# Attention: how the 32 couples of maxima of the next head are placed in the 16 groups of a head

## The reference, cut to what matters

```python
q = _split_heads(x @ Wq + bq, h)          # 16 heads of 64
k = _split_heads(x @ Wk + bk, h)
v = _split_heads(x @ Wv + bv, h)
pattern = jnp.einsum('bhid,bhjd->bhij', k, q) * scale
prob = jax.nn.softmax(pattern, axis=-2)
out = jnp.einsum('bhis,bhid->bhsd', prob, v)
...
return concat @ Wo + bo
```

## Time and profile before

| | us |
|---|---|
| median of 3 runs | 4512.2 |
| lowest and highest | 4512.07, 4518.56 |
| the profiled execution | 4520.46 |
| its span, first to last instruction | 4518.6 |
| start of the exponentials of head 0 and end of the last of head 31 | 108.4, 2910.8 |
| busy PE, DVE, ACT, POOL over the span | 4197.6, 3211.1, 3013.1, 2739.8 |

### The profile page before, as it was taken

One profiled execution on the slowest core, in us unless ns is written; L12 is line 12 of the kernel. 1 busy time (PEld: TensorE's weight loads), 2 busy tenths in 40 slices (PEclk: granted clock), 3 DMA queues, 4 the chain that ended last, 5 costly groups with the idle time before them and its releaser, 6 DMA issues.

```text
span 4518.6 us, 66192 instructions
## 1 busy us (share of the span) xinstructions
PE 4197.6 (93%) x23992; PEld 2418.2 (54%) x23992; DVE 3211.1 (71%) x4408; ACT 3013.1 (67%) x4371; POOL 2739.8 (61%) x1215
## 2 busy tenths in 40 slices
PE   7999999999999999999999999779998897999898
PEld 5444444444444444444444444357776675777675
DVE  5877878778778787787887788446664545666455
ACT  5877777778777787787786777646665444666442
POOL 2867778678766786786777777734553333454332
PEclk7999999999999999999999999979999998999999
DMA  2000000100010000001000100010000000000001
GB/s 82 23 21 29 21 21 15 35 21 15 21 33 16 21 24 25 21 15 35 20 16 21 34 16 16 10 61 1 1 1 21 18 1 19 1 1 1 1 1 38
DMA packets 100859, 89.47 MB, mean 20 GB/s; under 512 B 51092, under 2 KB 74088, under 8 KB 100584
## 3 DMA queue, kind: packets, MB, share of 16 engines
q1 hardware_dynamic: 100584, 85.75, 6.5%
HBM read 64.21 MB, written 4.46 MB: 15 GB/s over the span
## 4 chain that ended last, share of the span: by engine, by line
PE 42%; POOL 26%; DVE 12%; issue 11%; ACT 7%; POOLq 1%; DMA 1%; ACTq 0%; SPq 0%; DVEq 0%
POOL accp L780 23%; PE psum L1620 8%; PE psum L1790 6%; PE psum L1608 5%; PE psum L1572 5%; DVE mx L1216 4%; PE psum L1836 2%; PE psum L1920 2%; ACT lp L1029 2%; PE psum L1850 2%; POOL accp L776 2%; PE psum L1933 2%; PE psum L1827 2%; PE psum L1549 2%; PE psum L1557 1%
## 5 line engine op out<-in xcount | busy, mean ns | idle before, releaser
L780 POOL TENSOR_TENSOR accp<-accp,prob 128x1024 f32<-128x1024 f32 x704 | 1783.3, 2533 | 352.9 <-ACT prob L951 270.2
L1216 DVE TENSOR_REDUCE mx<-psum 128x1 f32<-128x512 f32 x1984 | 1276.9, 685 | 341.0 <-PE psum L1572 295.0
L951 ACT ACTIVATE prob<-psum 128x1024 f32<-128x1024 f32 x1024 | 1031.2, 1016 | 539.5 <-PE psum L1608 535.5
L1620 PE MATMUL psum<-prob,vv 128*64 128x512 f32 x4096 | 993.3, 606 | 0.0
L939 ACT ACTIVATE psum<-nm_all 128x1024 f32<-128x1024 f32 x832 | 855.8, 1029 | 26.3
L1572 PE MATMUL psum<-kh,qh 64*128 64x512 f32 x2048 | 494.6, 473 | 119.3 <-DVE mx L1216 113.4
L1572 PEld LDWEIGHTS psum<-kh,qh 64*128 64x128 f32 x2048 | 206.4, 185 | 607.0 <-DVE mx L1216 523.8
L811 POOL TENSOR_TENSOR lp<-lp,lrcp 128x1024 f32<-128x1024 f32 x128 | 242.6, 1895 | 448.6 <-DVE lrcp L1377 448.6
L1620 PEld LDWEIGHTS psum<-prob,vv 128*64 128x64 f32 x4096 | 248.7, 136 | 486.1 <-issue 391.1
L1608 PE MATMUL psum<-qh,kh 64*128 64x512 f32 x2048 | 419.8, 399 | 5.4 <-ACT psum L939 5.0
L1608 PE MATMUL psum<-ql,kh 64*128 64x512 f32 x2048 | 412.3, 391 | 0.0
(11 more groups left out here) (218 smaller groups left out, 6835.7 us busy)
## 6 DMA issues: line engine op xcount, KB each, us to landing
nm_all<-nm_rows SPq DMA_DIRECT2D x128, 256.0 KB, 3.7
kl<-kl SPq DMA_DIRECT2D x64, 256.0 KB, 3.8
wqk<-L_attn_Wq SPq DMA_DIRECT2D x64, 64.0 KB, 2.0
rot_l<-const_rot SPq DMA_DIRECT2D x2, 2048.0 KB, 8.6
out<-lpT SPq DMA_DIRECT2D x32, 128.0 KB, 1.7
wqkv_l<-L_ffn_wqkv SPq DMA_DIRECT2D x4, 768.0 KB, 9.7
w_l<-L_ffn_w SPq DMA_DIRECT2D x4, 618.0 KB
wqk<-L_attn_Wk SPq DMA_DIRECT2D x32, 64.0 KB, 2.1
```

The costliest lines, as they stand in the source:

```text
L780: pool.tensor_tensor(acc_p[cp][:], first[:], prob[kt % PRING][:], ALU.add).then_inc(pool_sum, 1)
L951: act.activation(prob[t % PRING][:], psum[:, S_BANK + 2 * (t % 2):S_BANK + 2 * (t % 2) + 2, :].rearrange("p a b -> p (a b)"), ACT.Exp, sca ...
L1216: dve.tensor_reduce(mx4[:, e, qt, c:c + 1], ps, AX_X, ALU.max).then_inc(ring_free, 1)
L1620: mm = pe.matmul(psum[j * DH:(j + 1) * DH, O_BANK, :], vv[:, kt, s * DH:(s + 1) * DH], prob[t % PRING][:, j * T:(j + 1) * T], start=(kt == ...
```

## The change

The weights go, and the places no longer depend on what else the head has to do. The counts are written out: two couples in most groups, one in group 0 and in group 11 (the first behind the middle sum), three in groups 6, 8, 13 and 14, none in group 15. All heads with maxima get

- 1 2 2 2 2 2 3 2 3 2 2 1 2 3 3 0

```diff
-        def max_places(outs):
-            weight = [4] * (GROUPS - 1) + [0]
-            weight[0] = 1
-            weight[SUM0_GROUP + 1:SUM0_GROUP + 3] = [0, 2]
-            for g in outs:
-                weight[g] = 3
-            return [-(-COUPLES * sum(weight[:g + 1]) // sum(weight)) for g in range(GROUPS)]
+        def max_places():
+            counts = [2] * (GROUPS - 1) + [0]
+            counts[0] = counts[SUM0_GROUP + 1] = 1
+            for g in (6, 8, GROUPS - 3, GROUPS - 2):
+                counts[g] = 3
+            assert sum(counts) == COUPLES
+            return [sum(counts[:g + 1]) for g in range(GROUPS)]
...
-            placed = max_places([*outs, *turns])
+            placed = max_places()
```

## The result

| | before | after |
|---|---|---|
| median, us | 4515.4 (4 runs) | 4629.1 (4 runs, 4623.2 to 4632.2) |
| span of the profiled execution | 4518.6 | 4627.9 |
| start of the exponentials of head 0, end of the last of head 31 | 108.4, 2910.8 | 108.8, 3020.4 |
| from one head to the next, even heads (median) | 88.2 | 91.7 |
| odd heads | 88.3 | 92.5 |

The changed kernel takes 1.025 times the time of the kernel before, interval 1.0237 to 1.0262. A fourth execution of the kernel before has moved its median from 4512.2 to 4515.4 us. All of the difference lies in the attention: between the two profiled executions it is 109.3 us from mark to mark of the third line, and 109.3 in the span.

The account below looks back on a forecast made before the run. PE bounds attention, and DVE's reductions where couples crowd. From 4512.2 us, +67 for the moved couples (+68, head 14 about -1) and +45 for the clock gave 4624 us (+2.5%), range 4545 to 4675.

Parts of the forecast that it names:

- Ahead of the middle sum: Attention up to group 10: three couples fewer bring its values earlier, -2.4 us in even heads, -1.0 in odd.
- The price of two twos in a row: Attention: two successive groups of two couples cannot keep 3.92 us each but take 4.16, 0.24 more.
- Behind the middle sum: Groups 11 and 12, all 30 heads: idle PE gap of 2.6 to 2.8 us, values of group 12 +3.2 us.
- Ahead of the turn: Group 14 gets a third couple, its tail waits for one more reduction: +1.2 us even heads, +0.3 odd.
- Sum without the clock: Attention: +2.0 us in each of 14 even heads and +2.5 in each of 16 odd ones, +68 us.
- The lower bound of the parts: Lowest total of the per-head terms in attention: 30 x 0, within bounds of 0 to 120 us.
- Head 14: This head already has a gap of 5.54 us and gets a shorter one: about -1 us.
- The clock: Behind the new gap PE's clock falls in half of 30 heads, 3 us each: +45 us, bounds 0 and 90.
- Rival C: Attention: all heads lose the clock behind the new gap, +90 us, 4669 us; chance 0.13.
- B: Attention: no head loses the clock behind the new gap, 4579 us; chance 0.24.
- E: Attention: POOL becomes the bound, adding at most 1 us a half, 4654 us or so; chance 0.08.
- D: Attention: spread pays in full, -3.6 us per head ahead of the sum, stall under 3.0; 4507 us; chance 0.13.

Follow-up runs that it names:

- e2: The changed kernel with the third couple of group 6 placed in group 5 instead; 4581.7 us, 1.0152 times the kernel before.
- e5: The kernel before with the third couples of groups 7 and 9 moved to groups 11 and 12, head 14 unchanged; 4577.3 us, 1.0139 times the kernel before.
- e4: The changed kernel with POOL's additions cut to the first 512 of 1024 columns; 4546.9 us, 1.0071 times the kernel before.
- e3: As e2, plus ten matmuls that nobody reads in group 12 ahead of its first couple; 4560.9 us, 1.0101 times the kernel before.

## Why the prediction was right, point by point

The point was 4624 us and the median is 4629. The mechanism is as forecast but for the clock, whose share came out near the forecast by luck. The parts, against the changed kernel with its idle stretches filled, where the clock takes nothing:

| per head, us | predicted | even | predicted | odd |
|---|---|---|---|---|
| values of group 10 | -2.4 | -2.46 | -1.0 | -0.77 |
| groups 11 and 12 | +3.2 | +3.01 | +3.2 | +3.01 |
| group 14 | +1.2 | +1.30 | +0.3 | +0.33 |
| whole head | +2.0 | +1.86 | +2.5 | +2.60 |

- *Ahead of the middle sum.* Right in both kinds of head, and for the reasons given. The gain of group 5 in even heads (3.91 instead of 5.05) is gone in group 6 (6.3 instead of 5.16), DVE's addition ending 1.1 us behind POOL's in both kernels. In odd heads the addition of tile 11 waits longer and group 6 takes 6.3. The price of two twos in a row was set at 4.16 a group; groups 2 to 5 of the odd heads took 3.91 to 4.84, 4.3 on average, and where two follow each other without a DVE addition in between, the second takes about 4.47 and the next 4.0. The mean was nearly right, the pattern was not seen. Group 10 shows it in both kinds of head (4.45).
- *Behind the middle sum.* The mechanism is as forecast, row by row. The gap is 2.50 us, not 2.6 to 2.8; the reciprocal starts at +3.2 (799.03 - 795.82), not +3.4.
- *Ahead of the turn.* Right in size and place: 5.21 in both kinds of head.
- *Sum without the clock.* +68 was predicted; 69 were measured with the fillers. The lower bound of the parts is not 0 as stated: -3.4 + 2.5 + 0.3 in odd heads gives -0.6 each, about -8 us in all. Nothing hung on it.
- *Head 14.* It gained 3.5 us, where -1 was predicted. What was left out is that the clock no longer falls there, which the prediction itself had priced at 3 us. With the fillers head 14 takes 98.8 us: the ten matmuls cost 2.9 us there, and they are in the 69.
- *The end of head 30.* The kernel before had a second long fall there, which the prediction did not see and which is gone in the changed kernel:

```profile
2842.15:2848.95 6.80, 4.87 (x18) 2.69 (x20) 2.85 (x1) 0.84 (x1) 1.79 (x1) 0.50 0.44 148
```

Head 30 took 87.9 us before and takes 88.1 now, while the other even heads got 3.5 longer.
- *The clock.* +45 was predicted for the 30 heads and 48 measured, but that agreement is owed to two errors that cancel. The step that failed is "I let it fall in half of the 30 heads: 15 x 3". There were 30 falls, in all heads with the new order but two (heads 0 and 14; head 29 had two). And each cost 1.6 us, not 3: the clock stayed low for 3.4 us here, where it had for 6.8 behind the gap in head 14 from which the price was taken. Also the place was wrong: 22 of the 30 came behind the wait of 1.43 us in group 6, a place for which the sum had priced the wait and not the clock; only 8 came behind the middle sum. Had the price of 3 us been right, the count would have given +90. With the two long falls that are gone, at 3 us each, the clock's net share is about 42 us; that is an estimate, and with the 68 it makes the 109 of the two profiles.
- *Rival C, all heads lose the clock,* is what happened in this profile by count, at half of its price. B (no fall) is the kernel with the fillers, 4581 against its 4579. E (POOL the bound) fell with POOL's halved additions, in spite of the chain of work. D fell with the cycles: it needed 3.6 us a head ahead of the middle sum, and 2.46 and 0.77 came; the stall cost 3.01, just over its limit of 3.0.
- The Trainium skill's page SBUF — State Buffer (the two separate sides), with its lock that one of VectorE and GpSimd holds for a whole instruction, agrees with the trace: DVE's addition took 2.42 us when it met POOL's and 1.24 when POOL's was half as long and all but over. The advice of the Trainium skill's page TensorE: Matmul & The Clock Gate (Why this matters for your kernels) to leave no long gap between bursts agrees with the fall behind the 5.54 us of head 14, but gaps that are short, 1.43 and 2.13 us, had a fall behind them too.

## What to carry to other kernels

In a ring whose places are freed in order by another engine, count on from every slow consumer by the number of places in the ring, three here: what is written there waits for it, and everything behind it in the producer's queue waits too. Spreading work evenly is no aim in itself; put it where the consumer is free, ahead of its long instructions and not right behind them. And price each new idle stretch on TensorE twice, for itself and for the clock behind it, also the stretches that seem too short to matter.

## What the runs showed of the hardware that was not expected

- **The clock falls behind short waits, and not always.** The same wait of 1.43 us in group 6 had a fall behind it in 22 of 30 heads of the changed kernel and in 2 of 30 when a couple elsewhere had moved. Waits of 2.5 us had one in 8 of 30 heads of the changed kernel and in 16 of 30 in e2, waits of 2.13 and 2.86 us in 28 of 30 (e5), waits of 2.13 with POOL's additions halved in 10 of 30 (e4). What else decides was not settled; the place in time may, since the stretch itself is alike to the hundredth. That is argued from the rows and no run tests it.
- **One fall cost 1.6 us** (48 us over 30; 25.7 over 16 from e2 to e3) and lasted 3.4 us, with the values at 3.63 us instead of 1.94.
- **Matmuls that nobody reads bought time.** Ten and five of them a head made the changed kernel 48 us faster.
- **A faster engine can meet another at the wrong moment.** With POOL's additions halved, group 14 took 6.1 us instead of 5.2, and DVE's addition in it 2.10 instead of 1.23.
